# Padding of expert regions one batch sooner, and three of four weight rests in the last stage

## The reference

```python
s = sigmoid(x2 @ Wg.T)                       # 3200 tokens x 16 experts, 4 groups of 4
group_mask = the 2 groups with the largest maximum
weights, idx = top 4 of s within these groups; weights *= 2.5 / sum(weights)
for e in range(16):
    we = sum(weights * (idx == e))
    h = silu(x2 @ W1[e].T + b1[e]) * (x2 @ W3[e].T + b3[e])
    y = y + (h @ W2[e].T + b2[e]) * we
x = x + tanh(g_ffn[1]) * y                   # x2 is the layer norm of x
```

## Time and profile before

| | |
|---|---|
| median of 3 runs | 2028.29 us (2022.79, 2028.29, 2030.18) |
| profiled execution | 2024.5 us |
| its span, first to last instruction | 2022.7 us |
| TensorE busy | 1878.4 us, 93% |
| VectorE busy | 1362.8 us, 67% |
| seam between the last dispatch and the first psG | 1652 to 1673 us of the span |

### The profile page before, as it was taken

How to read it: one execution, slowest core, us unless ns; L and a number is a source line. 1 busy time by engine, 2 the same in 40 slices (tenths; PEclk the granted TensorE clock), 3 DMA queues, 4 the chain that set the end, 5 groups by cost and what they waited for, 6 DMA issues and landing times. The chain is left out here.

```text
span 2022.7 us, 41825 instructions
## 1 busy us (share of the span) xinstructions
PE 1878.4 (93%) x11917; PEld 1379.8 (68%) x11917; DVE 1362.8 (67%) x4364; ACT 1053.8 (52%) x2664; POOL 1075.3 (53%) x1246
## 2 busy tenths in 40 slices
PE   5999999999999389999969999999999849999997
PEld 4888888888887278888835555555555536777665
DVE  4788888888887633322237787878888656666665
ACT  2554555454544323333238877887888733444443
POOL 2444445444444344554445777777777633555555
PEclk9999999999999589999979999999999959999999
DMA  4121111111115223333311211121111954555654
GB/s 140 50 56 30 42 28 42 29 42 29 42 30 208 74 40 53 53 51 51 54 35 32 58 52 54 50 58 54 56 48 56 300 194 86 97 93 93 98 93 67
DMA packets 138416, 142.35 MB, mean 70 GB/s; under 512 B 31658, under 2 KB 128658, under 8 KB 137816
## 3 DMA queue, kind: packets, MB, share of 16 engines
q1 hardware_dynamic: 98586, 92.90, 15.6%
q0 software_dynamic: 37888, 44.51, 13.8%
q10 hardware_dynamic: 1726, 2.28, 0.4%
HBM read 89.88 MB, written 51.94 MB: 70 GB/s over the span
## 5 line engine op out<-in xcount | busy, mean ns | idle before, releaser
L1956 POOL DMA_INDIRECT out<-y,xr x115 | 178.1, 1549 | 179.5 <-DVE y L1994 107.5
L925 POOL TENSOR_SCALAR prob<-prob,rc 100x363 f32<-100x363 f32 x256 | 147.4, 586 | 176.1 <-DVE rc L739 173.2
L634 ACT ACTIVATE prob<-psS,nm 100x361 f32<-100x361 f32 x256 | 141.4, 562 | 78.8 <-DVE nm L734 78.8
L1149 PE MATMUL psJ<-wkv,cTn 96*121 96x512 f32 x384 | 177.7, 600 | 0.0
L1692 POOL DMA_INDIRECT acc<-y,slots x57 | 90.4, 1585 | 136.8 <-DVE y L1750 121.9
L1609 POOL DMA_INDIRECT rows<-row,pos_of x128 | 134.5, 1051 | 44.1 <-issue 34.5
L1727 DVE TENSOR_TENSOR hid<-psU,gate 128x512 f32<-128x512 f32 x57 | 39.4, 692 | 159.6 <-PE psU L1844 159.6
L1594 POOL TENSOR_TENSOR rk<-rk,neghalf 121x12 f32<-121x12 f32 x64 | 127.0, 1985 | 5.3
L734 DVE TENSOR_REDUCE nm<-psS 100x2 f32<-100x722 f32 x128 | 115.9, 906 | 16.2 <-PE psS L523 8.1
L1978 DVE TENSOR_TENSOR pre<-psG,late 128x512 f32<-128x512 f32 x115 | 79.6, 692 | 68.2 <-PE psG L2082 68.1
L2038 ACT ACTIVATE x_hi<-psX 128x128 fp32r<-128x128 f32 x115 | 31.9, 277 | 179.0 <-PE psX L2069 179.0
(11 more groups left out here) (330 smaller groups left out, 5574.6 us busy)
## 6 DMA issues: line engine op xcount, KB each, us to landing
xr<-rows SPq DMA_DIRECT2D x115, 136.5 KB, 2.4
expert_w<-in_L_ffn_moe_w SPq DMA_DIRECT2D x8, 1024.0 KB, 15.5
late<-in_ctx SPq DMA_DIRECT2D x32, 181.5 KB
cT<-in_ctxT SPq DMA_DIRECT2D x32, 180.5 KB, 2.9
cT<-in_ctxT SPq DMA_DIRECT2D x64, 90.2 KB, 2.9
expert_w<-in_L_ffn_moe_w SPq DMA_DIRECT2D x8, 512.0 KB, 6.8
expert_w<-in_L_ffn_W1T SPq DMA_DIRECT2D x16, 256.0 KB, 6.5
expert_w<-in_L_ffn_W3T SPq DMA_DIRECT2D x16, 256.0 KB, 6.7
```

The lines of the kernel that those rows point to most:

```text
L634: s.activation(prob[:, q, 0:S], psS[0:N, h, 0:S], ACT.Exp, bias=nm[:, q:q + 1], accum_out=rs[:, q:q + 1]).then_inc(exp_done, 1)
L925: g.tensor_scalar(prob[:, q, :], prob[:, q, :], rc[:, q:q + 1], 1.0, ALU.mult, ALU.mult).then_inc(prob_done, 1)
L1149: mm = t.matmul(ph[0:rows, 0:cols], lhs, wt[:, k, :], start=k == 0, stop=k == 1)
L1956: g.indirect_dma_start(acc, bass.IndirectOffsetOnAxis(row_token[:, j % RING, :], 0), y[:, j % 4, :], None, compute_op=ALU.add).then_inc(sc ...
```

## The change

The padding of the regions is laid while the last batch is still in attention. The bases are copied to `base_i` behind the dispatch of batch 30. Batch 31 can then still add up to 100 rows to a region, so the copy is 128 + 99 = 227 rows long, and the scatters of batch 31 wait until all 16 copies have landed, as they write over part of them. SP issues two copies, then the last biases, then ten copies, then the store of the last batch; ACT issues four, in its last turn between the copies of the attention's output and the transposed rows. One of the four rests is made at the end of `attention1` and three at the start of `experts1`.

```diff
         def empty_tails(engine, which):
             for e in which:
-                end = engine.value_load(base_i[0:1, e:e + 1], min_val=e * REGION, max_val=e * REGION + TOKENS)
-                engine.dma_start(rows[bass.ds(end, P), :], rows[E1 * REGION:E1 * REGION + P, :]).then_inc(emptied, 16)
+                end = engine.value_load(base_i[0:1, e:e + 1], min_val=e * REGION, max_val=e * REGION + TOKENS - N)
+                engine.dma_start(rows[bass.ds(end, P + N - 1), :], rows[E1 * REGION:E1 * REGION + P + N - 1, :]).then_inc(emptied, 16)
...
@@ SP, in the loop over i @@
                     if i == B:
+                        s.wait_ge(plan, 1)
+                        empty_tails(s, range(0, 2))
                         s.wait_ge(o_mm, pairs * B)
                         load_bias(s, 6, E1)
+                        empty_tails(s, range(2, 12))
                     at(i - 1, store)
...
-                s.wait_ge(plan, 1)
-                empty_tails(s, range(0, E1 // 2))
@@ ACT, in the loop over i @@
                     at(i - 1, values, 1)
+                    if i == B:
+                        s.wait_ge(plan, 1)
+                        empty_tails(s, range(12, E1))
                     at(i + 1, q_transposed)
...
-                s.wait_ge(plan, 1)
-                empty_tails(s, range(E1 // 2, E1))
@@ VectorE @@
                     at(i - 1, y_dispatch)
+                    if i == B - 1:
+                        then(v.tensor_copy(base_i[:, :], c["base"][0:1, 0:E1]))
...
                 tile = c["tile"]
-                then(v.tensor_copy(base_i[:, :], c["base"][0:1, 0:E1]))
...
-                for q in range(2):
+                for q in range(1):
                     v.wait_ge(c["w1_high"], q + 1)
@@ GpSimd, scatter(b, k) @@
                         g.wait_ge(route, nth(ROUTE1, b, "w3"))
+                        if b == B - 1:
+                            g.wait_ge(emptied, 16 * E1)
@@ experts1, VectorE @@
-                for q in range(2, 4):
+                for q in range(1, 4):
```

More of the change, by code:

```diff
@@ L1509, in _, with then @@
                     v.memset(c["base"][:, e:e + 1], float(e * REGION))
+                steps = Count(plan)
+                def then(ins):
+                    n = steps.inc(ins)
+                    v.wait_ge(plan, n)
                 for i in range(-4, B + 2):
```

## The result

| | before | after |
|---|---|---|
| median, runs | 2028.4 us, 6 | 2042.28 us (2040.15 to 2043.46), 6 |
| ratio, 95% interval | | 1.0075 [1.0059, 1.0091], 15.2 us |
| span of the profiled execution | 2022.7 us | 2038.4 us |
| first psG of the last stage | 1673.18 us | 1690.28 us |
| from there to the end of the span | 349.5 us | 348.1 us |

The account below looks back on a forecast made before the run. It took the start of psG, the last stage's first large matmul, as the bound: tails landed at 1667.5 plus 14.5 us gives 1682.0, 8.8 us later. That gave 2033.3 by profile, 2037.1 by median; forecast 2036 us, range 2027 to 2043.

Parts of the forecast that it names:

- What bounds the kernel: At the seam from attention to the last experts stage, the start of psG moves the kernel's end by as much.
- One per 1.39 us on SP: SP's tail copies at the seam keep their old cadence of 1.39 us each; issues end at about 1656.4.
- The DMA engines have to carry it: At the seam the tails, biases and scatters load the busiest DMA engine with 26.0 us, 24.8 after dividing by 1.05.
- E: Moment all 16 tails have landed, releasing batch 31's scatters; forecast 1667.5, bounds 1663.4 to 1670.5, break-even 1658.7.
- dearer pieces: Rival, chance 0.25: 19 KB pieces beside the biases hold up the tails more than their bytes say; slower by over 10 us.
- 0.83 for the barrier: Between the blocks, VectorE goes on 0.83 us after the last arrival, taken from SP's last issue; part of 14.5 us.
- worth nothing by itself: VectorE's rests, 2+2 to 1+3 around the barrier: same work, at most the barrier's 0.55 us while the tails land late.
- 5.1 us in a hole of 5.4: ACT's four tails, 1.27 us each, fit between its copy of oT and xmT in the last batch.
- that its delay hides: Should ACT's burst make xmT late by 3 us, it hides, since GpSimd waits for the tails anyway.
- my rival: Tails hide, chance 0.12: 1.7 us less at best, or 1.3 us slower if ACT's burst takes 8.4 us.
- 13 pieces: Each 227-row tail is cut into 13 pieces of 19,068 bytes, on the same 13 engines, instead of 16 of 8,736.

Follow-up runs that it names:

- a2_len227: The kernel before with tails of 227 rows (13 pieces) at their old place; ratio 1.0030.
- d3_len129: The kernel before with tails of 129 rows (13 pieces) instead of 128 at their old place; ratio 1.0037.
- d1_228: The changed kernel with tails of 228 rows (14 pieces) instead of 227; one execution, 2043.08 us.
- d2_235: The changed kernel with tails of 235 rows (15 pieces) instead of 227; one execution, 2039.95 us.
- a3_240: The changed kernel with tails of 240 rows (16 pieces) instead of 227; ratio to the kernel before 1.0030.
- b2_tails_first: The changed kernel with tails of 240 rows and all twelve of SP's tails ahead of the last bias loads; ratio to the kernel before 1.0032.
- c2_bias_late: The changed kernel with the last pair of bias loads moved behind the sixth load of rows in the last stage; ratio to the kernel before 1.0061.
- a4_rests22: The changed kernel with the rests split 2+2 again instead of 1+3; ratio to the kernel before 1.0059.
- b4_act_later: The changed kernel with ACT's four tails moved behind its sigmoid exponent of the last batch; ratio to the kernel before 1.0075.
- c3_two_sooner_late: As b3_two_sooner, with the last pair of bias loads also moved behind the sixth load of rows in the last stage; ratio to the kernel before 0.9973.
- c4_before_late: The kernel before with only the last pair of bias loads moved behind the sixth load of rows in the last stage; ratio 0.9995.
- c1_227_first: The changed kernel, still 227 rows, with all twelve of SP's tails ahead of the last bias loads; ratio to the kernel before 1.0078.
- b3_two_sooner: The changed kernel with bases copied behind batch 29, 336-row tails all on SP ahead of the last four bias loads, rests 2+2; ratio to before 0.9994.
- b5_len240: The kernel before with tails of 240 rows (16 pieces) at their old place; ratio 1.0032.

## Why the prediction was wrong, step by step

- **What bounds the kernel: right.** One number, the start of psG, carries the result (17.1 us of it, 15.7 in the span, 15.2 by the ratio).
- **"One per 1.39 us on SP", the issues ending at 1656.4: this is the step that failed first, and the largest error.** I took the cadence from 16-piece copies and applied it to 13-piece ones. An issue costs 0.36 us more and the load of the next base 0.45 more: 2.2 us a tail. I had counted a cut in fewer pieces as a load on the DMA engines alone and never on the issuing engine (a2_len227, d3_len129, d1_228 and d2_235 show it). Ten copies behind the biases then took 25.9 us, of which 6.3 is the one issue right behind the loads in 2,560 small pieces (a3_240 against b2_tails_first; c2_bias_late). Issues ended at 1670.4, 14 us later than assumed.
- **"The DMA engines have to carry it", E = 1667.5: failed as the cause, 5.7 us short.** E was 1674.03 - 0.86 = 1673.2, and it followed the last issue by 3.7 us, at a DMA share of about 0.4. Where the engines are full the sum of their work was close: in a3_240 the share is 0.89 to 1.12 in every 2.5 us from 1647.5 to 1665, and the same working (15 tails at 0.90 us a piece on all 16 engines, 8.1 and 2.1 beside them, 23.7 / 1.05 = 22.6 us) puts E 25.8 us behind the first tail; it came 25.5 behind. That is one case, and its SP was held by a long issue as well. The rival "dearer pieces" had the right time and the wrong mechanism: the large pieces were not slow to move (ACT's 52 in after kept its queue busy for 6.4% of 16 engines over 38 us, 0.75 us each; 0.92 by the same sum in a2_len227; 1.05 was forecast), they were slow to be issued, at any size.
- **"0.83 for the barrier": failed, 2.8 us short.** I took it from SP's last issue. Before, GpSimd arrived with SP; behind a late scatter its own drain is the term: 3.6 us in all from the last scatter to VectorE's next rest. So the stretch from E to psG was 17.1 us and not 14.5.
- **The split 1+3 "worth nothing by itself": half right.** At the old place it costs 1.3 us by the trace and nothing the time can tell; in the changed kernel the third rest behind the barrier is 2.2 us of the 17.1. I had it in the sum (3 x 2.24), but called the split worthless, and held that it can't cost more than 0.55 us while E is late. With E late it costs a whole rest (a4_rests22).
- **ACT's burst, "5.1 us in a hole of 5.4": failed; that its delay hides: right.** Four issues took 8.4 us and xmT came 3.35 us late, hidden behind the wait for E (b4_act_later). The 8.4 us stand in my rival too, but for another reason, the biases beside them, so the match is luck. ACT's issue takes 1.29 us for 13 pieces with no biases near (a2_len227), and four copies in 16 pieces are issued in 4.4 us (b2_tails_first):

```profile
1640.78 4.40 ACTq L1048 DMA_DIRECT2D rows<-rows  x4
```

- **13 pieces: right.** The DMA view of 1638 to 1643 us has 39 packets of which 13 are small: 26 large ones for two tails.

```profile
DMA packets 39, 0.50 MB, mean 99 GB/s; under 512 B 13, under 2 KB 13, under 8 KB 13
```

5.7 for E and 2.6 for what follows it are the 8.3 us between 8.8 forecast and 17.1 measured.

## What to carry to other kernels

Before a transfer's length is changed, look at how many pieces it is cut in, and price the issuing engine as well as the carrying: here 129 rows cost more than 128 by 7 us, and 240 cost less than 227 (8.7 us by the trace at the new place, 3.2 at the old one). Where work leaves the end of a block, list every engine's drain by its end, not only the one the chain of waits names; the next one may be 0.1 us behind. A transfer moved ahead of small-pieced loads or behind them moves those loads too, and they land on whatever was quiet before.

## What the runs showed of the hardware that I had not expected

- A DRAM-to-DRAM copy in 13, 14 or 15 pieces holds SP 0.88 to 0.93 us at its issue, one in 16 pieces 0.53, whatever the pieces' size (8.7 to 22.9 KB for 16, 10.8 and 19.1 KB for 13); ACT 1.28 to 1.40 against 0.53. The next load of a register from memory takes 0.72 us instead of 0.27 on SP.
- GpSimd's drain at the end of a block ends 3.3 us behind its last scatter when the DMA queues are quiet (after, c2_bias_late, c3_two_sooner_late), 4.2 us at a share of 0.41 (d3_len129), and 5.5 to 9.6 us when the tails or the biases fill them (c4_before_late, a2_len227, c1_227_first, b3_two_sooner, before, b5_len240). The pair b3_two_sooner and c3_two_sooner_late, which differ in the place of the biases alone, shows it best: 5.8 and 3.3.
- An issue on SP right behind the two loads of 2,560 pieces took 5.3 to 6.3 us in five kernels (after, a4_rests22, a3_240, d1_228, d2_235) and 2.6 in one in which ACT issued its copies later (b4_act_later); where no tail stood behind them, the store of x took 3.5 (b2_tails_first, c1_227_first). That this is a wait for room in the queue is argued from its standing behind the biases wherever they are and its absence where they are moved out (c2_bias_late), not shown.
